# A four-layer graph network on one core: the incidence matrix formed before the transposes, and the transposed adj kept once as fp32

## The chip, the core and the metric

The kernel runs on one core of one Trainium2 chip. TensorE (PE) multiplies, VectorE (DVE) and ScalarE (ACT) do the elementwise work, GpSimd (POOL) does small powers, two reductions over the partitions and the DMAs that add, and SyncE (SP) issues the other DMAs. The metric is the device time of one execution in microseconds (us), the median of several runs.

## What is computed

`x` is 2048x256 in fp32, `adj` is 2048x2048 and sparse, with its diagonal set and entries between 0.05 and 1. Four layers run one after another, each as `x = x + layer(relu(layernorm(x)), adj)`:

```python
# layer 0
deg = sum(adj.T, axis=1); norm = deg**-0.5 [:, None] * adj.T * deg**-0.5 [None, :]
y = norm @ (h @ weight) + bias
# layer 1
head = (adj > 0) / max(sqrt(sum((adj > 0)**2, -1)), 1e-12)
inc = adj + head
y = (inc @ h) / sum(inc, -1)
# layer 2, four heads
ht = (h @ W) per head
e = leaky_relu(src[:, :, None] + dst[:, None, :], 0.01) + adj
y = mean over heads of softmax(e) @ ht
# layer 3
y = relu(adj @ (max(sign(h), 0) @ sign(weight).T))
```

## The kernel before

The 2048 rows are 16 blocks of 128 (`NB`); one block of `adj` against all 16 blocks of columns is a row block. Each product in fp32 is made of fp16 products of high and low parts: a high part is a cast by ACT (times 256 for `adj`), a low part is one instruction of DVE that computes value minus high part. A product of one 128x128 piece takes three matmuls (high·high, high·low, low·high). The order on each engine is the order of the code; semaphores join the engines; nothing is reordered by a scheduler. A block of "loop" code (`Fori`) is run by the engine's sequencer; the rest is unrolled.

- **Load and degrees** (about 0 to 70 us): `adj` comes in as 32 halves of row blocks, ACT and DVE cut it into parts in `nat`, PE sums the degrees.
- **Layer 0** (about 72 to 166 us): for each of 16 row blocks PE runs 48 matmuls (L542 to L544, L552 to L554 for the first two); DVE adds the bias (L1116), takes the sum from PSUM into `x` (L1119), then statistics, relu and the low part `h1_lo` (L1104); ACT makes `h1_hi` (L832) after POOL's power (L438). In the first half DVE also takes a running maximum of `adj` (L1113), from which POOL's reduction over the partitions (L442) gives the shift of the exponential.
- **Layer 1** (166 to 339 us): SP loads `adj` again into `stage` (L330). Per row block and per group of four column blocks (`transpose_group`) PE turns four 128x128 pieces in fp32 (L574); ACT makes the fp16 high part (L848) and `exp(adj - max)` in fp32 (L850) out of PSUM; DVE makes the low part (L1167) and the mask `adj > 0` (L1171). PE then runs, for each of 16 column blocks, five matmuls (`products1`, L594 to L599): three for `adj @ h` and two for `mask @ h`, in two accumulators with a column of ones for the row sums. The sums are combined after the products (`row_counts`, `row_sums`, L1192 to L1208). SP writes the fp16 parts (`adj_t_parts`, L336) and the exponential (`exp_adj_t`, L339) to DRAM, 1 MB each per row block. `h2_transposes` and `scores` (L609, L618) of earlier blocks stand among the products.
- **Between layers 1 and 2** (339 to 398 us): PE forms `ht` for all 16 blocks (`ht_block`, L663, 192 matmuls of 512 columns), ACT and DVE make its high and low parts (L911, L1292). From the scores come the factors `u` and `w`; `u` goes to DRAM and back, spread over all partitions (L359, L362). Behind those loads on SP stands `load_e` (L374), which loads the exponential of four row blocks as 16 pieces into `e_in`.
- **Layer 2** (398 to 741 us): four quarters of the rows times four heads (a "group") times 16 column blocks, 256 steps in all. A step: DVE makes the numerators (L1277), ACT their fp16 high part (L983), DVE the low part (L1282), PE 12 matmuls (L704 to L706). `prob`, `p_hi` and `p_lo` have four slots, so ACT may start on a step when PE is done with the step four earlier (`p_used`). Heads are scaled by ACT (L937) and added to `x` by a DMA of POOL (L460). During quarters 1 to 3 PE, ACT also prepare `xw` of layer 3 (`binary_turn`, `binary_product`).
- **Layer 3** (741 to 805 us): 16 row blocks of 32 matmuls (L745, L746) on the fp16 parts that SP loads back from `adj_t_parts` (L393, L403) into four slots `at3`; DVE adds the result into `x` (L1345), SP writes it out.

## Time and profile before

| what | us |
|---|---|
| median of 3 runs | 808.45 |
| lowest and highest | 804.88, 808.72 |
| the profiled execution, its own time | 806.78 |
| its span (first to last instruction) | 805.0 |
| PE busy in the span | 762.2 (95%) |
| DVE busy | 630.1 (78%) |
| ACT busy | 397.5 (49%) |
| POOL busy | 56.9 (7%) |

The profile is one execution. A matmul's own duration (about 273 ns) overlaps with those around it, so its busy times by line add up to more than the span; what a matmul costs is read from the starts of neighbours. The chain of waits names, for each moment, the instruction that the end of the program waited for.

### The profile page before, as it was taken

The page shows a single profiled execution, that of the slowest core. Times are in us where ns is not written, and L with a number is a line of the kernel's source. Part 1 is how long each engine was busy: PE and PEld are TensorE (multiplying, and loading weights), DVE is VectorE, ACT ScalarE, POOL GpSimd, SP SyncE. Part 2 cuts the span into 40 slices and gives each one's busy share as a digit, 9 for nine tenths or more (in the row PEclk, how much of TensorE's full clock was granted, in tenths as well). Part 3 has the DMA queues.
Part 4 walks back from the last instruction along what each step waited for, and adds up shares of the span by engine and source line. Part 5 has one row for each costly group of instructions (what it writes and reads, how often), then busy time and mean ns, then how long its engine had stood idle before and what let it go on. Part 6 is the DMA issues. An engine that isn't in the chain of part 4 may idle for free.

```text
span 805.0 us, 19016 instructions
## 1 busy us (share of the span) xinstructions
PE 762.2 (95%) x7064; PEld 646.7 (80%) x7064; DVE 630.1 (78%) x1313; ACT 397.5 (49%) x772; POOL 56.9 (7%) x83
## 2 busy tenths in 40 slices
PE   3898998899999999879799999999999999999898
PEld 3665887789999999734488888888888888888687
DVE  6787884867777777646899999999999999996111
ACT  3995100255555555236555555855576555754200
POOL 2002221101101011100000000000000000000000
PEclk9998999999999999979999999999999999999999
DMA  9885002068888887417601181116311490112494
GB/s 336 283 286 177 1 0 104 31 237 292 284 284 298 286 288 239 164 27 211 181 2 28 32 231 28 28 28 180 84 27 28 109 299 18 24 27 80 155 399 178
DMA packets 96716, 120.54 MB, mean 150 GB/s; under 512 B 3537, under 2 KB 82065, under 8 KB 92433
## 3 DMA queue, kind: packets, MB, share of 16 engines
q1 hardware_dynamic: 94496, 111.85, 42.4%
q0 software_dynamic: 2160, 7.87, 5.1%
q8 instruction: 42, 0.69, 0.4%
q14 instruction: 18, 0.14, 0.1%
HBM read 76.15 MB, written 35.68 MB: 139 GB/s over the span
## 4 chain that ended last, share of the span: by engine, by line
PE 76%; DVE 8%; issue 6%; ACT 4%; SPq 3%; DMA 2%; POOL 0%; DVEq 0%; POOLq 0%; ACTq 0%
PE ps L704 14%; PE ps L706 14%; PE ps L705 14%; PE ps L594 4%; PE ps L574 4%; PE ps L596 4%; PE ps L599 3%; PE ps L597 3%; PE ps L595 3%; PE ps L745 3%; PE ps L746 3%; SPq L362 2%; ACT arena L776 1%; DVE arena L1052 1%; DVE arena L1113 1%
## 5 line engine op out<-in xcount | busy, mean ns | idle before, releaser
L704 PE MATMUL ps<-arena 128*128 128x257 f16 x1024 | 279.9, 273 | 2.9 <-DVE arena L1292 2.9
L706 PE MATMUL ps<-arena 128*128 128x257 f16 x1024 | 279.4, 273 | 0.0
L705 PE MATMUL ps<-arena 128*128 128x257 f16 x1024 | 279.2, 273 | 0.0
L983 ACT ACTIVATE arena<-arena 128x512 f16<-128x512 f32 x252 | 158.6, 629 | 136.7 <-PE ps L706 134.7
L1277 DVE SCALAR_TENSOR_TENSOR arena<-arena,w_j 128x512 f32<-128x512 f32 x256 | 190.1, 743 | 0.9 <-DMA arena<-exp_adj_t 0.9
L1282 DVE TENSOR_TENSOR arena<-arena 128x512 f16<-128x512 f32 x256 | 176.3, 689 | 6.1 <-ACT arena L983 5.7
L704 PEld LDWEIGHTS ps<-arena 128*128 128x128 f16 x1024 | 99.9, 98 | 15.9 <-DVE arena L1292 3.4
L705 PEld LDWEIGHTS ps<-arena 128*128 128x128 f16 x1024 | 100.4, 98 | 12.5
L706 PEld LDWEIGHTS ps<-arena 128*128 128x128 f16 x1024 | 99.8, 98 | 12.9
L1167 DVE SCALAR_TENSOR_TENSOR arena<-ps,arena 128x512 f16<-128x512 f32 x64 | 44.0, 687 | 39.9 <-ACT arena L850 39.6
L594 PE MATMUL ps<-arena 128*128 128x257 f16 x256 | 70.3, 275 | 0.0
L599 PE MATMUL ps<-arena 128*128 128x257 f16 x256 | 69.9, 273 | 0.0
L596 PE MATMUL ps<-arena 128*128 128x257 f16 x256 | 69.7, 272 | 0.0
L597 PE MATMUL ps<-arena 128*128 128x256 f16 x256 | 69.7, 272 | 0.0
L595 PE MATMUL ps<-arena 128*128 128x256 f16 x256 | 69.4, 271 | 0.0
L542 PE MATMUL ps<-arena 128*128 128x256 f16 x224 | 61.6, 275 | 2.5 <-DVE x L1119 2.5
L848 ACT ACTIVATE arena<-ps 128x512 f16<-128x512 f32 x64 | 38.1, 596 | 48.1 <-PE ps L574 46.3
L544 PE MATMUL ps<-arena 128*128 128x256 f16 x224 | 61.5, 275 | 0.0
L543 PE MATMUL ps<-arena 128*128 128x256 f16 x224 | 61.5, 275 | 0.0
L745 PE MATMUL ps<-arena 128*128 128x256 f16 x256 | 56.1, 273 | 3.4 <-DMA arena<-adj_t_parts 2.7
L746 PE MATMUL ps<-arena 128*128 128x256 f16 x256 | 56.1, 273 | 0.0
L663 PE MATMUL ps<-arena 128*128 128x512 f16 x192 | 45.9, 404 | 5.0 <-DVE arena L1292 3.4
(148 smaller groups left out, 1082.5 us busy)
## 6 DMA issues: line engine op xcount, KB each, us to landing
arena<-in_adj_dram SPq DMA_DIRECT2D x64, 512.0 KB, 5.5
adj_t_parts<-arena SPq DMA_DIRECT2D x16, 1024.0 KB, 4.6
exp_adj_t<-arena SPq DMA_DIRECT2D x16, 1024.0 KB, 7.8
arena<-exp_adj_t SPq DMA_DIRECT2D x64, 256.0 KB, 4.5
arena<-adj_t_parts SPq DMA_DIRECT2D x16, 1024.0 KB, 7.6
x<-arena POOLq DMA_DIRECT2D x15, 512.0 KB, 5.0
arena<-u_rows SPq DMA_DIRECT2D x4, 1024.0 KB, 14.7
x<-in_x_dram SPq DMA_DIRECT2D x4, 512.0 KB, 5.5
```

The source lines that it names most:

```text
L594: mm(ps[:, 2 * b, 0:DE], at[:, b, 0, j, :], h1_hi[:, j, 0:DE], start=s, stop=False)
L595: mm(ps[:, 2 * b, 0:D], at[:, b, 0, j, :], h1_lo[:, j, :], start=False, stop=False)
L596: mm(ps[:, 2 * b, 0:DE], at[:, b, 1, j, :], h1_hi[:, j, 0:DE], start=False, stop=e)
L597: mm(ps[:, 2 * b + 1, 0:D], mask[:, b, j, :], h1_lo[:, j, :], start=s, stop=False, skip_group_check=True)
L599: ins = mm(ps[:, 2 * b + 1, 0:DE], mask[:, b, j, :], h1_hi[:, j, 0:DE], start=False, stop=e, skip_group_check=True)
L704: mm(ps[:, bank, 0:DE], hi, ht_hi[:, head, j, 0:DE], start=s, stop=False)
L705: mm(ps[:, bank, 0:DE], hi, ht_lo[:, head, j, 0:DE], start=False, stop=False)
L706: ins = mm(ps[:, bank, 0:DE], lo, ht_hi[:, head, j, 0:DE], start=False, stop=e)
L745: mm(ps[:, k, 0:D], at3[:, k, 0, j, :], xw[:, j, :], start=(j == 0), stop=False)
L983: nc.scalar.activation(p_hi[:, j % 4, :], prob[:, j % 4, :], copy).then_inc(p_hi_done, 1)
L1277: v.scalar_tensor_tensor(prob[:, j % 4, :], u_bc[:, h, q * (QB * P):(q + 1) * (QB * P)], w_j[:, j, h:h + 1], e_in[:, j, :], ALU.max, ALU.m ...
L1282: v.tensor_tensor(p_lo[:, j % 4, :], prob[:, j % 4, :], p_hi[:, j % 4, :], ALU.subtract).then_inc(p_lo_done, 1)
```

## The change

- **Layer 1.** SP loads whole rows (`rows`, four buffers of 8 KB per partition). DVE counts the positive entries of a row with one instruction over 2048 columns (`count`: mask and count), POOL takes count^-0.5 (`inverse_count`), and DVE forms `inc = mask * c + adj` with a second instruction over 2048 columns (`fill`), in natural layout. PE turns both `inc` and `adj` in fp32 (eight pieces a group instead of four). ACT makes the fp16 high part of `inc` and copies the turned `adj` in fp32; DVE makes the low part of `inc` (`inc_low`). PE runs three matmuls per column block instead of five, in one accumulator. The row sums take one reciprocal and one instruction.
- **What goes to DRAM.** One fp32 tensor `adj_t`, 1 MB per row block, instead of the fp16 parts and the exponential.
- **Layer 2.** `load_e` loads `adj_t` (512 columns a piece, 16 pieces a quarter); for quarter 0 it stands on SP right behind the end of layer 1 and ahead of the `u` loads. ACT applies the exponential in place (`exp_adj`, 64 instructions of 128x512): four before the exponentials of the scores, six among the `ht` parts, the others among the steps (head 3 of the quarter before, and head 0). The scaling of the last head of a quarter moves from steps 4 to 7 to steps 10 to 13 of the next head 0. The first head's products wait for `ht_lo` column block by column block.
- **Layer 3.** Its fp16 parts are made by ACT (`at3_high`, 128x2048) and DVE (`at3_low`, 128x2048) from `adj_t`: row blocks 0 and 1 inside head 2 of quarters 1 and 2, block 2 and 3 about the end of layer 2, the others inside layer 3.
- **`ht`.** `ht_block` uses three PSUM slots in turn instead of two; blocks 0 to 2 run before the scores' results are back.
- **Layer 0.** The bias is added to `x` by four accumulating DMAs of POOL (from DRAM, spread over partitions) instead of 16 instructions of DVE. `count` and `fill` of the first two row blocks stand in layer 0 (blocks 8 to 11); the transposes of row block 0 stand behind its last four blocks.
- The loops of layers 0, 1, `ht` and 3 are unrolled.

```diff
-    at_dram = nc.dram_tensor("adj_t_parts", (NB, P, 2 * N), F16, kind="Internal").ap()
-    e_dram = nc.dram_tensor("exp_adj_t", (NB, NB, P, P), F32, kind="Internal").ap()
+    adjt_dram = nc.dram_tensor("adj_t", (NB, P, N), F32, kind="Internal").ap()
...
+            sp.wait_ge(l1_ps, NB)
+            load_e(0)
...
             sp.wait_ge(ut_done, 1)
             sp.dma_start(u_dram.rearrange("t h n -> (t h) n"), up_t[0:HEADS * NB, :]).then_inc(u_out, 16)
...
+            pool.wait_ge(relu0, NB)
+            for p in range(4):
+                nc.gpsimd.dma_start(x[:, XP * p:XP * p + XP, :],
+                                    b0_d.partition_broadcast(P).unsqueeze(1).broadcast_to([P, XP, D]),
+                                    accum_op=ALU.add).then_inc(bias_in[p], 16)
...
+            def transpose_group(t, g):
+                n = 4 * t + g
+                if g == 0:
+                    pe.wait_ge(rows_in[t % 4], 16 * (t // 4 + 1))
+                    pe.wait_ge(filled, t + 1)
+                if n >= 2:
+                    pe.wait_ge(adjt_copied, n - 1)
+                    pe.wait_ge(inc_lo_done, n - 1)
...
-                    mm(ps[:, 2 * b, 0:DE], at[:, b, 0, j, :], h1_hi[:, j, 0:DE], start=s, stop=False)
-                    mm(ps[:, 2 * b, 0:D], at[:, b, 0, j, :], h1_lo[:, j, :], start=False, stop=False)
-                    mm(ps[:, 2 * b, 0:DE], at[:, b, 1, j, :], h1_hi[:, j, 0:DE], start=False, stop=e)
-                    mm(ps[:, 2 * b + 1, 0:D], mask[:, b, j, :], h1_lo[:, j, :], start=s, stop=False,
-                       skip_group_check=True)
-                    ins = mm(ps[:, 2 * b + 1, 0:DE], mask[:, b, j, :], h1_hi[:, j, 0:DE], start=False, stop=e,
-                             skip_group_check=True)
+                    mm(ps[:, bank, 0:DE], inc_parts[:, b, 0, j, :], h1_hi[:, j, 0:DE], start=s, stop=False)
+                    mm(ps[:, bank, 0:D], inc_parts[:, b, 0, j, :], h1_lo[:, j, :], start=False, stop=False)
+                    ins = mm(ps[:, bank, 0:DE], inc_parts[:, b, 1, j, :], h1_hi[:, j, 0:DE], start=False, stop=e)
...
+            def exp_adj(q, j):
+                if j % TG == 0:
+                    act.wait_ge(e_loaded[j // TG], 16 * QB * (q + 1))
+                nc.scalar.activation(e_in[:, :, j, :], e_in[:, :, j, :], ACT.Exp, bias=amax[:, 2:3]
+                                     ).then_inc(e_exp, 1)
...
+            h2_turned(NB - 2)
+            h2_high(NB - 1)
+            h2_turned(NB - 1)
+            for j in range(4):
+                exp_adj(0, j)
             act.wait_ge(d_shift, 1)
...
+            def count(t):
+                dve.wait_ge(rows_in[t % 4], 16 * (t // 4 + 1))
+                v.tensor_scalar(mask[:, t % 2, :], rows[t % 4], 0.0, NORM_EPS ** 2, ALU.is_gt, ALU.add,
+                                accum_out=cnt[:, t:t + 1]).then_inc(counted, 1)
+
+            def fill(t):
+                dve.wait_ge(counted, t + 1)
+                dve.wait_ge(c_done, t + 1)
+                if t >= 2:
+                    dve.wait_ge(t_ps, 4 * (t - 2) + 4)
+                v.scalar_tensor_tensor(inc[:, t % 2, :], mask[:, t % 2, :], c_row[:, t:t + 1], rows[t % 4],
+                                       ALU.mult, ALU.add).then_inc(filled, 1)
...
+            def at3_high(i, part, parts=4):
...
+                    if i >= 4:
+                        act.wait_ge(o_ps, i - 3)
...
-                if h == 0 and j % TG == 0:
-                    dve.wait_ge(e_loaded[j // TG], 16 * TG * (q + 1))
+                if h == 0:
+                    dve.wait_ge(e_exp, NB * q + j + 1)
```

On DVE one steady row block of layer 1 read before as below (lines 1167 and 1171 are the low part and the mask of a group, and stand four times in a block):

```order
L1192 TENSOR_SCALAR row_n<-ps 128x1
L1194 TENSOR_SCALAR row_n<-ps 128x1
L1167 SCALAR_TENSOR_TENSOR arena<-ps,arena 128x512
L1171 TENSOR_SCALAR arena<-ps 128x512
L1200 SCALAR_TENSOR_TENSOR row_n<-ps,row_n 128x1
L1202 RECIPROCAL row_n<-row_n 128x1
L1203 TENSOR_SCALAR row_n<-row_n 128x1
L1205 TENSOR_SCALAR row_n<-row_n 128x1
L1206 SCALAR_TENSOR_TENSOR x<-ps,row_n,x 128x256
L1208 SCALAR_TENSOR_TENSOR x<-ps,row_n,x 128x256
```

And so it reads after, on the same engine at the same place (L1234 is `inc_low`, L1220 `count`, L1228 `fill`):

```order
L1234 SCALAR_TENSOR_TENSOR arena<-ps,arena 128x512
L1220 TENSOR_SCALAR arena,cnt<-arena 128x2048
L1234 SCALAR_TENSOR_TENSOR arena<-ps,arena 128x512
L1275 RECIPROCAL row_n<-ps 128x1
L1276 SCALAR_TENSOR_TENSOR x<-ps,row_n,x 128x256
L1228 SCALAR_TENSOR_TENSOR arena<-arena,c_row 128x2048
L1234 SCALAR_TENSOR_TENSOR arena<-ps,arena 128x512
```

The four masks of 512 columns are gone, two instructions of 2048 columns have come in, and the chain of small instructions is shorter by five.

On SP, from the end of layer 1 to layer 2, before:

```order
L336 DMA adj_t_parts<-arena 128x4096
L339 DMA exp_adj_t<-arena 128x16x128
L359 DMA u_rows<-arena 64x128
L362 DMA arena<-u_rows 128x16x128 x4
L374 DMA arena<-exp_adj_t 128x4x128 x64
```

And after, at the same place:

```order
L346 DMA adj_t<-arena 128x2048 x5
L377 DMA arena<-adj_t 128x512 x16
L386 DMA u_rows<-arena 64x128
L389 DMA arena<-u_rows 128x16x128 x4
L395 DMA arena<-adj_t 128x2048 x2
L377 DMA arena<-adj_t 128x512 x48
```

The 16 loads for the first quarter have moved from behind the `u` loads to ahead of them.

## Rows read from the trace of the kernel before

**Rows 1.** The page, parts 1 and 6: engines, then DMA issues, us to landing last.

```profile
PE 762.2 (95%) x7064; PEld 646.7 (80%) x7064; DVE 630.1 (78%) x1313; ACT 397.5 (49%) x772; POOL 56.9 (7%) x83
...
arena<-exp_adj_t SPq DMA_DIRECT2D x64, 256.0 KB, 4.5
...
x<-arena POOLq DMA_DIRECT2D x15, 512.0 KB, 5.0
```

**Rows 2.** Busy time by stretch: length, each engine (instructions), PE clock, DMA share, GB/s.

```profile
72.00:165.90 93.90, 88.34 (x788) 77.98 (x787) 72.91 (x214) 17.18 (x36) 16.59 (x18) 0.98 0.14 52
165.90:339.10 173.20, 172.81 (x1662) 156.25 (x1659) 124.71 (x355) 87.62 (x151) 17.62 (x31) 1.00 0.82 272
339.10:398.10 59.00, 47.36 (x214) 20.53 (x211) 38.10 (x97) 30.66 (x75) 1.53 (x3) 0.91 0.54 143
398.10:740.50 342.40, 342.40 (x3122) 303.92 (x3123) 332.01 (x534) 201.86 (x396) 13.20 (x15) 1.00 0.29 73
740.50:805.00 64.50, 57.94 (x529) 50.78 (x526) 8.79 (x22) 8.32 (x28) 0.00 (x0) 1.00 0.61 228
```

**Rows 3.** The chain in order of time, in layer 1: start, us, what.

```profile
214.95 0.49 PE ps L574 x4
...
225.91 0.49 PE ps L574 x4
...
325.08 0.11 PE ps L594
325.19 0.11 PE ps L595
```

**Rows 4.** Groups by line and shape, DVE and ACT: busy, mean ns, idle before.

```profile
L1167 DVE SCALAR_TENSOR_TENSOR arena<-ps,arena 128x512 f16<-128x512 f32 x64 | 44.0, 687 | 39.9 <-ACT arena L850 39.6
L850 ACT ACTIVATE arena<-ps,amax 128x512 f32<-128x512 f32 x64 | 43.8, 684 | 0.0
...
L1139 DVE CUSTOM_DVE_ANT_0 arena<-arena 128x256 f32<-128x256 f32 x16 | 6.8, 422 | 0.4
...
L1240 DVE SCALAR_TENSOR_TENSOR arena<-arena 128x2048 f16<-128x2048 f32 x1 | 2.3, 2292 | 0.5 <-ACT arena L877 0.5
...
L877 ACT ACTIVATE arena<-arena 128x2048 f16<-128x2048 f32 x1 | 1.9, 1910 | 0.0
...
L1030 DVE TENSOR_SCALAR arena<-arena 128x512 f16<-128x512 f32 x1 | 0.4, 420 | 0.0
```

**Rows 5.** Timeline in layer 0: start, us, engine, line, what, idle before.

```profile
135.33 0.48 DVE L1104 SCALAR_TENSOR_TENSOR arena<-arena,rstd 128x256 f16<-128x256 f32 x1 [9.46 <-ACT arena L832]
```

**Rows 6.** Waits in layer 0: who waited for whom, us in total, times, longest.

```profile
PE ps L574 <- DVE arena L1171: 3.1, 2, 2.6
...
PE ps L542 <- DVE x L1119: 2.5, 2, 2.1
```

**Rows 7.** The chain in order of time, from layer 1 to layer 2.

```profile
339.12 0.17 DVE row_n L1192
...
372.19 4.61 SPq L374
...
379.82 6.08 DMA arena<-exp_adj_t
...
398.10 0.28 PE ps L704
```

**Rows 8.** Timeline of PE in the same stretch: start, us, engine, line, what.

```profile
354.67 33.50 PE L663 MATMUL ps<-arena 128*128 128x512 f16 x144 [1.73 <-DVE arena L1292]
```

**Rows 9.** Timeline of DVE and of ACT in layer 2, columns as in rows 5.

```profile
560.85 0.75 DVE L1277 SCALAR_TENSOR_TENSOR arena<-arena,w_j 128x512 f32<-128x512 f32 x1
561.56 0.69 DVE L1282 TENSOR_TENSOR arena<-arena 128x512 f16<-128x512 f32 x1
...
562.22 0.63 ACT L983 ACTIVATE arena<-arena 128x512 f16<-128x512 f32 x1 [0.69 <-PE ps L706]
```

**Rows 10.** Layer 3: the longest piece of the chain that is no matmul.

```profile
754.90 5.01 DMA arena<-adj_t_parts
```

More of the change, by code:

```diff
@@ L408, in _ @@
+            for t in range(NB - 8, NB):
+                store_out(t)
             sp.wait_ge(out_sent, 16 * NB)
@@ L453, in _ @@
+            for t in range(NB):
+                if t + 2 < NB:
+                    inverse_count(t + 2)
+                if t >= 1:
+                    inverse_root2(t - 1)
+            inverse_root2(NB - 1)
             pool.wait_ge(dmax_part, 1)
@@ new lines, in _ @@
+            pe.wait_ge(deg_copied, 1)
+            for g in range(NB // TG):
+                layer0(NB - 4 + g)
+                transpose_group(0, g)
+            for t in range(NB):
+                for g in range(NB // TG):
+                    if t + 1 < NB:
+                        transpose_group(t + 1, g)
+                    products1(t, g)
+                    if g == 0 and t >= 2:
+                        h2_transposes(t - 2)
+                    if g == 2 and t >= 2:
+                        if t == 2:
+                            pe.wait_ge(wa_done, 1)
+                        scores(t - 2)
@@ new lines, in ht_block @@
+            def ht_block(t):
+                for half in range(2):
+                    if t >= 3:
+                        last = max(k for k in range(t) if HT_SLOT[k] == HT_SLOT[t])
+                        pe.wait_ge(ht_lo_done, HEADS * last + 2 * half + 2)
+                    n = 0
+                    for ha, wb in ((0, w2_hi), (0, w2_lo), (1, w2_hi)):
+                        for c in range(DC):
+                            ins = mm(ps[:, HT_SLOT[t] + half, :], h2_t[:, ha * DC + c, t * P:(t + 1) * P],
+                                     wb[:, c, 512 * half:512 * half + 512], start=(n == 0), stop=(n == 5))
+                            n += 1
+                    ins.then_inc(ht_ps, 1)
@@ L677, in _ @@
+            nc.tensor.transpose(ps[0:HEADS * NB, 6, 0:P], up_i[:, :, :].rearrange("p t h -> p (t h)"),
                                 ident[:, :]).then_inc(ut_ps, 1)
-            with nc.tensor.Fori(1, NB // 2) as i:
-                ht_block(i, False)
+            for t in range(3, NB):
+                ht_block(t)
             def head_products(q, head, first):
@@ L1240, in _ @@
-            v.scalar_tensor_tensor(w2_lo, w2_f, W_SCALE, w2_hi, ALU.mult, ALU.subtract).then_inc(w2_lo_done, 1)
-            with nc.vector.Fori(1, NB // 2) as i:
-                for b in range(2):
-                    layer1(i, b, True)
-            for b in range(2):
-                row_counts(NB - 2 + b, b)
-                row_sums(NB - 2 + b, b)
-                row_norm(NB - 2 + b, b)
-                h2_low(NB - 2 + b, b)
+            for t in range(NB):
+                more = t + 1 < NB
+                if more:
+                    inc_low(t + 1, 0)
+                if t == 0:
+                    w2_a(1, (2, 3))
+                    w2_a_parts()
+                if t + 2 < NB:
+                    count(t + 2)
+                if more:
+                    inc_low(t + 1, 1)
+                if t >= 1:
+                    row_sums(t - 1)
+                if t + 2 < NB:
+                    fill(t + 2)
+                if more:
+                    inc_low(t + 1, 2)
+                if t >= 1:
+                    row_norm(t - 1)
+                if more:
+                    inc_low(t + 1, 3)
+                if t >= 1:
+                    h2_low(t - 1)
+                if t == 0:
+                    dve.wait_ge(w2_hi_done, 1)
+                    v.scalar_tensor_tensor(w2_lo, w2_f, W_SCALE, w2_hi, ALU.mult, ALU.subtract
+                                           ).then_inc(w2_lo_done, 1)
```

789 lines of the change are left out of this document (409 added, 380 removed).

## The prediction

> **What bounds the kernel now.** I read the table of stretches first, then the chain of waits in order of time, then the timelines of the places where the chain leaves PE. PE is busy 762.2 of 805.0 us [rows 1]. By stretch, PE fills layer 1 (172.8 of 173.2 us) and layer 2 (342.4 of 342.4), and has holes in layer 0's end, between layers 1 and 2 (47.4 of 59.0) and in layer 3 (57.9 of 64.5); its clock is full in the three long stretches [rows 2]. So a gain comes either from fewer PE instructions in layer 1 or from closing those holes. In layer 2 DVE is busy 332.0 of 342.4 us and ACT 201.9 [rows 2]: DVE has little to give, ACT much. One matmul starts 0.11 us after its neighbour, four fp32 transposes take 0.44 to 0.49 us of the chain, also 0.11 each, and a row block of layer 1 is 225.91 - 214.95 = 10.96 us long [rows 3]. Check: 80 matmuls and 16 transposes are 96 x 0.11 = 10.6, and `h2_transposes` and `scores` make the rest.
>
> The sum is made against the profiled execution (806.78 us, of which 1.8 lie outside its span); the median of the runs shown is 1.7 above it.
>
> **Layer 1, PE's own work.** Per row block 32 matmuls go and 16 transposes come: 48 x 0.11 + 32 x 0.11 + 0.35 = 9.15, with the bubble that the block of before shows 9.2 us. 10.96 - 9.2 = 1.76, times the 15 blocks that have transposes beside them, is 26.4; the last block has none and saves 32 x 0.11 = 3.5. Together -29.9.
>
> **Layer 1, is DVE fast enough?** Instructions that follow without a wait start about 0.08 us closer than they are long, so a low part of 512 costs 0.61 [rows 4]. Four of them are 2.44. `fill` is a two-input instruction of 2048 with a per-partition factor; L1240, the same without the factor, took 2.29 [rows 4], so 2.3. The reciprocal and the sum into `x` are 0.6, the norm 1.0, `h2_low` 0.4. `count` has no row of its kind: an SBUF-sourced TENSOR_SCALAR of 512 took 0.42 (L1030, 0.52 ns an element and 0.15 fixed), which gives 1.2 us for 2048; the accumulating L1139 took 0.42 for 256, an element per cycle, which gives 2.3 with its read-out [rows 4]. I take 2.3, as the row that also accumulates. DVE then needs 9.05 us a block against PE's 9.15: even. Walking the order of the code, PE's turn of a group waits for the low part two groups earlier and each low part for PE's turn and ACT's cast; with both near 9.15 the walk finds no gap in a steady block, and a POOL power (0.55 us) lies under the `inc_low` between `count` and `fill`. ACT has four casts and four copies of 0.6 and 1.1 more, 5.9 of 9.15. At the start it does not close: in block 0 DVE has in addition two pairs of `w2_a` and `w2_lo` (4.6 us) and no slack, so PE waits about 1.3 us twice. I add 2.6 for that and 1.0 for jitter. If `count` takes 1.2 us, these 3.6 shrink to about 1; if waits leave DVE 0.5 us longer a block, they grow to 10. Layer 1 in all: -29.9 + 3.6 = -26.3 (-29 to -19).
>
> The Trainium skill (VectorE: DVE Perf Modes, section "The perf-mode tier table (the rule you actually need)") lists 1227 ns for a fp32 `tensor_scalar` of 2048 elements in SBUF and says nothing of one that accumulates; by it the sum would be some 2.5 us lower than mine.
>
> **Layer 0.** Removed on DVE: 16 bias adds of 0.42 us, which PE did not wait for. Added: `count` and `fill` twice, in blocks 8 to 11. There DVE sits out POOL's reduction, 9.46 us until 135.33 [rows 5], and PE lost 2.1 us to it, waiting for the sum of block 10 [rows 6]. Now `fill(0)` (2.3) stands in front of that sum, less two bias adds (0.8): a wait of 3.6 instead of 2.1. The 16 more transposes of row block 0 cost 1.8 here. Against this PE's two waits for the low parts and masks of the first turned groups go (3.1 us before [rows 6]), and with them holes of 1.7 about them in which nothing was issued. I count -1.5 for the start of layer 1's products (165.9 before), between -4 and +4. The four bias DMAs start when POOL's powers for the degrees are done, and an adding DMA of this size takes 5.0 us to land [rows 1]; PE's first two sums need 96 x 0.11 = 10.6 us from about the same moment. Covered; if the first lands late, it costs what it is late.
>
> **Between layers 1 and 2.** Layer 1 ended at 339.1, the first product of layer 2 was at 398.1: 59.0 us [rows 7]. The chain ran through the `u` loads, `load_e` behind them (372.2), its landing at 385.9, and then 12 us of numerators and `ht_low` [rows 7]. Afterwards `load_e` is issued at the end of layer 1, 33 us earlier, so it goes off this chain, and PE's `ht` work comes next: 192 matmuls. From the end of layer 1 (E) I count blocks 0 to 2 of `ht`, two `h2_transposes` and `scores` until E+9.4; the return of the scores' factors, which now waits behind four exponentials (4 x 0.68 [rows 4]) that wait for the first 1 MB of `adj_t` (about 6.5 us after E), E+12; then 156 matmuls. 144 took 33.5 us there, with the clock's mean at 0.91 in this stretch [rows 2, 8], so 36 us: E+48. DVE meanwhile follows, and its last `ht_low` and first numerators leave PE waiting some 2.5 us in the first steps. So 50.5 instead of 59.0: -8.5 (-12 to 0; zero if the loads or the factors come as late as before).
>
> **Layer 2.** PE's 12 matmuls a step make 1.32 us, and DVE and ACT keep step with it [rows 9]. ACT waited 0.69 us before each `p_hi` [rows 9]. An exponential from PSUM took 0.684 [rows 4]; two ACT instructions in a row overlap by 0.1, so a step with one is 0.53 + 0.6 = 1.15 of 1.32. It is hidden by ACT's wait, and `p_hi` is only late when a load is late; the loads of the next quarter are issued when its columns are free, five to six steps (7 us) before their exponential, against 4.5 us to landing for 256 KB [rows 1]. DVE gets 8 low parts of 0.61 us for layer 3, four in a row: 2.4 us late, within the three steps that PE has ready. I take +1 for the stretch (0 to +10).
>
> **Layer 3.** PE waited 5.0 us for a load of `adj_t_parts` that could not be issued earlier [rows 10]. Now blocks 2 to 5 are loaded during the last head. The new late one is the cast of block 4: ACT waits for block 0 to leave its slot (`o_ps`), then 1.91 (L877's time), then DVE 2.3 (L1240) [rows 4], while PE has 3 x 0.88 us of work left: a stall of 1.8. Afterwards DVE needs 2.65 a block and ACT 1.9 against PE's 3.5. So -3.2 (-5 to +2).
>
> **Sum.** -1.5 - 26.3 - 8.5 + 1 - 3.2 = -38.5; 806.8 - 38.5 = 768.3. With -1 for the short form of `count`, which I hold possible, I forecast **767 us**.
>
> **Rivals.**
> 1. *DVE bounds layer 1.* If the lag between turn, cast and low part isn't hidden when DVE and PE are both full, a block takes 10.2 us, 15 x 1.0 more: 782. For it: DVE's 9.05 of 9.15. Against: in the walk each low part is ready 0.3 us or more before DVE comes to it.
> 2. *Layer 2 starts no earlier relative to E.* The factors wait behind the exponentials and PE's clock falls in the hole: 776. For it: before, the clock's mean was 0.91 there [rows 2].
> 3. *The exponentials are not hidden in layer 2.* Each adds its own 0.68 to its step through the chain numerators, `p_hi`, low part, next step: 64 x 0.68 = 43.5, which gives 811, slower than before. It decides from 0.6 us each on. Against: 0.69 us of ACT's wait in each step [rows 9].
> 4. *PE's clock falls in layer 1.* At 1.2 GHz, half the clock, a block would be up to 9.2 us longer; five blocks of 16 take the whole gain (above 807), all would give 900. In the block of before 16 of 96 PE instructions were transposes and the clock was 1.00 [rows 2, 3]; now 32 of 80 are. The Trainium skill (TensorE: Matmul & The Clock Gate, section "Part 4: PE-mode transpose") says that transposes do not count as PE being busy in the same way; the trace of before, at full clock with fewer of them, neither shows nor excludes it for this mixture.
> 5. *Better than counted.* `count` short, no wait at the start of layer 1, layer 2 begun at E+47: 759.
>
> **Chances.** Forecast 0.58 (762 to 774), rival 1: 0.12, rival 2: 0.14, rival 3: 0.03, rival 4: 0.03, rival 5: 0.10. The range 756 to 786 leaves out rivals 3 and 4 and the far ends of the others. Faster by over 0.5% (about what a measurement of this kernel can tell from no change) 0.94, within 0.5% 0.01, slower 0.05.
>
> **What would show it.** Layer 1's row blocks 9.1 to 9.5 us apart; `count` 1.2 or 2.3 us; PE idle before the turned groups under 5 us in the stretch; E near 311; first product of layer 2 near E+48 and its steps 1.32 us; one stall of about 2 us in layer 3 before block 4. A block pitch of 10 and more, or PE waiting for low parts in steps with an exponential, would make the prediction wrong.

## The result, and the profile after

The changed kernel takes **771.71 us** (median of four runs, 769.29 to 773.97) where the kernel before took 807.4 beside it: a ratio of 0.956, 95% interval 0.952 to 0.960. Measured again later, on one chip with three of the experiments, it was 0.954 (0.951 to 0.957). Its profiled execution has a span of 768.8 us against 805.0, so 36.2 us went. The forecast of 767 is 4.7 below the median; the median lies inside the range that the forecast gave for its own case (762 to 774).

I cut both profiled executions at five events on PE and DVE (degrees read by DVE, first and last product of layer 1, last product of layer 2, end). Times and changes are in us:

| stretch | before | after | change | forecast |
|---|---|---|---|---|
| start to degrees | 69.4 | 66.2 | -3.2 | 0 |
| to the first product of layer 1 | 96.5 | 93.8 | -2.7 | -1.5 |
| layer 1 | 173.2 | 149.4 | -23.8 | -26.3 |
| end of layer 1 to end of layer 2 | 401.3 | 396.0 | -5.3 | -7.5 |
| rest | 64.6 | 63.4 | -1.2 | -3.2 |

The table of stretches of the kernel after (columns: from and to, then busy us and instructions of PE, of PE's weight loads, of DVE, ACT and POOL, then PE's granted clock, DMA share, GB/s) answers to [rows 2]:

```profile
72.00:160.00 88.00, 85.49 (x783) 76.62 (x781) 67.53 (x188) 13.55 (x28) 14.39 (x22) 1.00 0.36 73
160.00:309.40 149.40, 144.81 (x1383) 130.18 (x1381) 135.14 (x252) 80.60 (x152) 17.09 (x30) 1.00 0.60 198
309.40:360.60 51.20, 44.60 (x215) 19.97 (x213) 31.21 (x80) 33.43 (x79) 0.97 (x2) 0.93 0.59 165
360.60:705.40 344.80, 342.63 (x3122) 303.63 (x3121) 337.47 (x554) 245.05 (x470) 13.06 (x15) 1.00 0.29 79
705.40:768.80 63.40, 57.91 (x530) 50.94 (x527) 39.24 (x36) 30.92 (x40) 0.00 (x0) 1.00 0.55 200
```

In layer 1 PE was full before (172.8 of 173.2); now it is busy 144.8 of 149.4 and DVE 135.1, so something holds PE up. The granted clock stayed at 1.00 there (full speed, 2.4 GHz), with 32 transposes to 48 products in a row block: rival 4 did not happen. Between the layers PE's clock is 0.93 on the mean.

One steady row block of layer 1 on DVE, from its timeline (start, us, engine, line, operation, names and shapes, and in brackets the idle time before it with what ended it); it answers to the sum of durations made from [rows 4]:

```profile
221.32 2.27 DVE L1220 TENSOR_SCALAR_CACHE_REDUCE arena<-arena 128x2048 f16<-128x2048 f32 x1
223.52 0.08 DVE L1220 DVE_READ_ACCUMULATOR arena<-arena 128x1 f32 x1
...
224.72 2.34 DVE L1228 SCALAR_TENSOR_TENSOR arena<-arena,c_row 128x2048 f32<-128x2048 f16 x1
...
228.59 0.68 DVE L1234 SCALAR_TENSOR_TENSOR arena<-ps,arena 128x512 f16<-128x512 f32 x1
229.71 0.48 DVE L1297 SCALAR_TENSOR_TENSOR arena<-arena,row_n 128x256 f16<-128x256 f32 x1 [0.44 <-ACT arena L878]
230.19 0.69 DVE L1234 SCALAR_TENSOR_TENSOR arena<-ps,arena 128x512 f16<-128x512 f32 x1
230.80 2.27 DVE L1220 TENSOR_SCALAR_CACHE_REDUCE arena<-arena 128x2048 f16<-128x2048 f32 x1
```

From one `count` to the next it is 230.80 - 221.32 = 9.48 us. The whole idle time is the 0.44 us ahead of L1297, `h2_low`, which waits for ACT's high part L878, and that for POOL's power of the norm. The waits of DVE and PE in layer 1 as the waits view adds them up (total, times, longest):

```profile
DVE arena L1297 <- ACT arena L878: 7.0, 15, 1.0
PE ps L603 <- DVE arena L1234: 3.1, 3, 1.8
```

Between the layers the chain of waits reads (start, us, what):

```profile
316.68 0.28 DVE dmax L1335
316.96 5.09 issue
322.05 0.40 POOL dmax L488
322.47 0.24 DVE w_j L1339
...
325.26 30.38 PE ps L680 x132
355.66 0.85 ACT arena L943 x2
```

The maximum of d was ready for POOL at 316.96, and POOL's reduction over the partitions began 5.09 us later, though POOL waited for nothing that the profile shows. PE's turn of the scaled scores (L699) waited for it:

```profile
PE ps L699 <- DVE up_i L1343: 4.8, 1, 4.8
PE ps L730 <- DVE arena L1364: 2.2, 2, 1.6
```

### The profile page after: what moved, and what is told of

It reads as the page before. It is cut to its first block, busy times and chain, and to the rows that moved or that the text cites. A ratio compares the mean times of both kernels' runs of the same rounds, so it can differ in the third digit from the quotient of the medians.

```text
span 768.8 us, 16799 instructions
## 1 busy us (share of the span) xinstructions
PE 729.3 (95%) x6808; PEld 619.3 (81%) x6808; DVE 667.2 (87%) x1207; ACT 458.7 (60%) x861; POOL 57.1 (7%) x87
## 4 chain that ended last, share of the span: by engine, by line
PE 72%; DVE 3%; issue 1%; ACT 1%; POOL 0%; ACTq 0%
PE ps L730 14%; PE ps L732 14%; PE ps L731 14%; PE ps L680 5%; PE ps L772 4%; PE ps L773 3%; PE ps L627 3%; PE ps L629 3%; PE ps L628 3%; PE ps L603 3%; PE ps L607 3%; PE ps L641 1%; DVE arena L1228 1%; DVE arena L1371 1%; DVE arena L1234 0%
## 5 line engine op out<-in xcount | busy, mean ns | idle before, releaser
L730 PE MATMUL ps<-arena 128*128 128x257 f16 x1024 | 279.9, 273 | 2.2 <-DVE arena L1364 2.2
L732 PE MATMUL ps<-arena 128*128 128x257 f16 x1024 | 279.4, 273 | 0.0
L731 PE MATMUL ps<-arena 128*128 128x257 f16 x1024 | 279.2, 273 | 0.0
L1037 ACT ACTIVATE arena<-arena 128x512 f16<-128x512 f32 x252 | 158.5, 629 | 95.6 <-PE ps L732 53.2
L627 PE MATMUL ps<-arena 128*128 128x257 f16 x256 | 70.3, 274 | 0.0
L629 PE MATMUL ps<-arena 128*128 128x257 f16 x256 | 69.7, 272 | 0.0
L628 PE MATMUL ps<-arena 128*128 128x256 f16 x256 | 69.4, 271 | 0.0
L574 PE MATMUL ps<-arena 128*128 128x256 f16 x224 | 61.1, 273 | 2.5 <-DVE x L1188 2.5
L576 PE MATMUL ps<-arena 128*128 128x256 f16 x224 | 61.1, 273 | 0.0
L575 PE MATMUL ps<-arena 128*128 128x256 f16 x224 | 61.1, 273 | 0.0
L772 PE MATMUL ps<-arena 128*128 128x256 f16 x256 | 56.1, 273 | 2.5 <-DVE arena L1404 1.8
L773 PE MATMUL ps<-arena 128*128 128x256 f16 x256 | 56.1, 273 | 0.0
L858 ACT ACTIVATE arena<-arena,rstd 128x256 f16<-128x256 f32 x16 | 8.2, 510 | 64.1 <-POOL rstd L458 64.1
L1234 DVE SCALAR_TENSOR_TENSOR arena<-ps,arena 128x512 f16<-128x512 f32 x64 | 43.8, 685 | 2.9 <-ACT arena L869 2.9
L915 ACT ACTIVATE arena<-arena,amax 128x512 f32<-128x512 f32 x64 | 45.0, 708 | 1.3 <-DMA arena<-adj_t 1.3
L680 PE MATMUL ps<-arena 128*128 128x512 f16 x192 | 43.8, 390 | 1.1 <-DVE arena L1371 1.1
```

Source lines behind the costliest of these rows:

```text
L627: mm(ps[:, bank, 0:DE], inc_parts[:, b, 0, j, :], h1_hi[:, j, 0:DE], start=s, stop=False)
L628: mm(ps[:, bank, 0:D], inc_parts[:, b, 0, j, :], h1_lo[:, j, :], start=False, stop=False)
L629: ins = mm(ps[:, bank, 0:DE], inc_parts[:, b, 1, j, :], h1_hi[:, j, 0:DE], start=False, stop=e)
L680: ins = mm(ps[:, HT_SLOT[t] + half, :], h2_t[:, ha * DC + c, t * P:(t + 1) * P], wb[:, c, 512 * half:512 * half + 512], start=(n == 0), st ...
L730: mm(ps[:, bank, 0:DE], hi, ht_hi[:, head, j, 0:DE], start=s, stop=False)
L731: mm(ps[:, bank, 0:DE], hi, ht_lo[:, head, j, 0:DE], start=False, stop=False)
```

## The experiments

Each was run beside the kernel before on one chip, and its ratio is to that. e2 issues the first load of layer 2 later, e3 finishes h2 later in layer 1, e6 leaves `count` out, e16 leaves only its summing out, e9 adds two matmuls a column block, e11 issues the first bias DMA earlier, e12 is e2, e3 and e11 together, e10 is e2 and e3; e14 leaves exponentials out and e15 makes them twice. All these start from the changed kernel; e8 alone starts from the kernel before, with its load issued earlier. Since the stretch up to the degrees moves by itself (below), single stages are compared by the events of the profiled executions. "Row block" is the distance of two row blocks of layer 1 (empty where I did not read it), "way to layer 2" is from the last product of layer 1 to the first of layer 2; the last column is from the last product of layer 2 to the end of the span.

| kernel | ratio to before (95%) | row block | layer 1 | way to layer 2 | layer 2 | rest |
|---|---|---|---|---|---|---|
| before | 1 | 10.96 | 172.9 | 59.3 | 342.1 | 64.8 |
| after | 0.956 (0.952 to 0.960) | 9.48 | 149.3 | 51.3 | 344.6 | 63.6 |
| e2 | 0.949 (0.947 to 0.952) | | 149.3 | 45.3 | 344.6 | 63.6 |
| e3 | 0.948 (0.945 to 0.950) | 9.22 | 145.6 | 49.4 | 344.6 | 63.6 |
| e6 | 0.945 (0.942 to 0.948) | 9.20 | 142.6 | 51.1 | 344.6 | 63.5 |
| e8 | 0.996 (0.995 to 0.998) | | 172.9 | 58.3 | 343.7 | 64.9 |
| e9 | 1.016 (1.014 to 1.017) | 12.70 | 197.7 | 50.8 | 344.6 | 63.5 |
| e11 | 0.955 (0.954 to 0.957) | | 149.3 | 50.1 | 344.6 | 63.6 |
| e12 | 0.946 (0.944 to 0.948) | | 145.7 | 45.7 | 344.6 | 63.5 |
| e14 | 0.952 (0.950 to 0.955) | | 149.3 | 51.3 | 344.6 | 63.6 |
| e15 | 0.977 (0.975 to 0.978) | | 149.3 | 51.0 | 365.9 | 63.6 |
| e16 | one run, 766.7 us | 9.20 | 144.0 | 50.6 | 344.6 | 63.6 |
| e10 | 0.942 (0.940 to 0.944) | 9.22 | 145.7 | 45.5 | 344.6 | 63.6 |

(Layer 1 is given here from the start of its first to the start of its last product, so 0.1 less than above.)

### The changed kernel once more

> The changed kernel as it is, so that the kernels of this group have it beside them on the same chip: 0.956 of the kernel before, within 0.004, about 773 where the kernel before takes 808.8. It also shows how far the end of the load stage moves by itself between executions (the first product of layer 1 came at 160.0 in its first profiled run, and at 159.8 to 162.8 in three variants that leave that stage alone).

Measured: 0.9539, median 772.56 us. The degrees were read at 67.2 and not 66.2, and layer 1 began at 162.3; from there to the end every stage is within 0.4 us of the first profile. So stages can be compared to a few tenths between executions, and the time up to layer 1 only to 2 or 3 us. In ten profiles, of the changed kernel and of its variants that leave the load stage alone, the degrees came at 66.2 to 68.5; of the kernel before there are two, 69.4 (the profile of [rows 1]) and 66.9 (e8). The 3.2 us of the first row of the table is therefore most likely no effect of the change. From the degrees to layer 1 these ten profiles took 93.4 to 95.8 us, against 96.5 and 96.8 (e8) before, so of the second row's 2.7 us only 0.7 to 3.1 can be said.

### Is POOL's late reduction the load's doing? (e2)

```diff
             sp.wait_ge(l1_ps, NB)
+            sp.wait_ge(dmax_all, 1)
             load_e(0)
```

The load is of 4 MB, and not of 2 as the expectation says. And it is not one thing that moves: ACT's first four `exp_adj`, which need this load, move with it, from ahead of the scores' exponentials to among the `ht` parts.

> The changed kernel with one thing moved: the load of the first exponentials' input (2 MB by SyncE's queue) is issued only when GpSimd has given the maximum of d over all partitions, and ScalarE's first exponentials stand some three blocks later. Nothing is left out. In the changed kernel GpSimd stood 10.2 us between its last power and that maximum while this load was landing, against 7.5 us in the kernel before, where it was not. Theory (the load slows GpSimd's change of program): the gap falls to 6 to 7.5 us, the first product of layer 2 comes 3 to 4 us earlier after the end of layer 1, and the time falls by 3 to 4 us against the changed kernel (to about 768). Rival (the gap is GpSimd's own, whatever the queues do): the gap stays at 10 us and the time within 1 us; the exponentials may then even come late for the first product, and cost up to 2 us.

POOL's timeline of the kernel after, and then of e2:

```profile
311.22 0.59 POOL L463 TENSOR_TENSOR row_n<-row_n,neg_half 128x1 f32<-128x1 f32 x1 [4.49 <-DVE row_n L1287]
322.05 0.39 POOL L488 PARTITION_ALL_REDUCE dmax<-dmax  x1 [10.24 <-issue]
```

```profile
313.62 0.58 POOL L464 TENSOR_TENSOR row_n<-row_n,neg_half 128x1 f32<-128x1 f32 x1 [4.50 <-DVE row_n L1286]
320.11 0.39 POOL L489 PARTITION_ALL_REDUCE dmax<-dmax  x1 [5.91 <-DVE dmax L1334]
```

Between power and reduction POOL stood 10.24 us, and now 5.91, as in layer 0 (5.96 in the kernel after). (The 7.5 us that the expectation names for the kernel before ended when DVE's maximum came, so they are no price of POOL's.)

All profiles of the changed kernel and its variants fall in two groups: with the load in flight 8.4 to 10.2 us in nine (DMA share 0.82 to 0.89 over the gap), without it 5.9 to 6.2 in three (e2, e10, e12; DMA share 0.00). A load does not always do this. In layer 0 of the kernel before a load ran too, at a share of 0.52, and the gap was 6.1. In e8 (below) the same 4 MB were issued 1.2 us after the power, the share over the gap was 0.60, and the reduction began at 348.62, 0.1 us after the maximum was ready: POOL's own part was 7.5 us at most there. ACT's four exponentials, which e8 does not have at this place, began at 317.21 in the kernel after, inside POOL's gap; no run moves them alone, so that it is the load and not they is likely and not shown. What POOL does in that time (it changes from a power to a reduction) the profile does not name; POOL's queue shows two MODIFY_POOL_CONFIG at the start of the gap (312.0 in the kernel after, 314.4 in e2).

The way to layer 2 fell by 6.0 us, more than the 4.4 that PE's wait lost (4.8 to 0.4). The rest is in the `ht` products that follow. Tables of stretches, after and then e2, over the hole and over the same 132 products:

```profile
309.40:325.00 15.60, 9.26 (x59) 4.27 (x56) 4.78 (x20) 6.46 (x15) 0.97 (x2) 0.90 0.79 270
325.00:355.50 30.50, 30.24 (x133) 13.39 (x134) 21.82 (x52) 23.66 (x58) 0.00 (x0) 0.94 0.59 139
```

```profile
311.80:323.00 11.20, 9.13 (x59) 4.24 (x56) 4.71 (x20) 3.85 (x11) 0.97 (x2) 1.00 0.10 20
323.00:352.00 29.00, 28.68 (x133) 13.05 (x134) 21.81 (x52) 25.33 (x62) 0.00 (x0) 1.00 0.75 234
```

The granted clock was 0.90 and 0.94 of full speed on the mean with PE's wait of 4.8 us, and 1.00 without it. Cut finer, it was 0.50 (1.2 GHz) from 322 to 327 and 1.00 from 329, with PE idle from 318.9 to 323.7 and for 1.1 us more until 325.3. The products took 30.4 us of the chain and then 28.7. The wait cost 4.4 us and the clock behind it another 1.7. The exponentials in their later place put nothing on the way to layer 2. Against the changed kernel the time fell by 0.5 to 0.7%, some 5 us.

### Does the 0.44 us wait for `h2_low` matter? (e3)

`h2_low(t - 1)`, which stood last in DVE's turn t, behind its fourth `inc_low`, is now `h2_low(t - 2)` behind `count(t + 2)`; ACT's `h2_high`, PE's `h2_transposes` and `scores` move later likewise.

> The changed kernel with the finishing of each row block of h2 (high part on ScalarE, low part on VectorE, transposes on TensorE) put one to three groups later in each engine's order of layer 1, so that VectorE no longer stands 0.44 us a block for ScalarE's high part behind GpSimd's power. Nothing is left out. Theory (VectorE bounds the block of 9.48 us: 9.05 busy and 0.44 of wait): the block falls to 9.1 to 9.2 us, 16 blocks give 4 to 5 us, about 767. Rival (TensorE bounds it, 8.86 us of matmuls and what its sequencer adds): the block stays at 9.4 or more, and the time within 1 us.

The row blocks are 9.22 us apart and layer 1 is 3.7 us shorter. PE's transposes of h2 in the timeline of PE (one line a block) show the distance:

```profile
205.21 0.39 PE L641 MATMUL ps<-ident,arena 128*128 128x128 f16 x4
214.43 0.39 PE L641 MATMUL ps<-ident,arena 128*128 128x128 f16 x4
223.65 0.39 PE L641 MATMUL ps<-ident,arena 128*128 128x128 f16 x4
```

So the theory held for layer 1. Another 1.9 us came on the way to layer 2, where POOL's gap was 8.6 us and PE's wait 2.6 instead of 4.8 us; I had not expected that, and no run shows why the gap was shorter.

### What lies under DVE's limit? (e6, e16, e9)

e6 leaves `count` out from row block 2 on, e16 only its summing:

```diff
-                v.tensor_scalar(mask[:, t % 2, :], rows[t % 4], 0.0, NORM_EPS ** 2, ALU.is_gt, ALU.add,
-                                accum_out=cnt[:, t:t + 1]).then_inc(counted, 1)
+                    v.tensor_scalar(mask[:, t % 2, :], rows[t % 4], 0.0, None, ALU.is_gt)
+                    v.tensor_copy(cnt[:, t:t + 1], cnt[:, t - 2:t - 1]).then_inc(counted, 1)
```

> The changed kernel with VectorE's count of the incidence entries of a row (2.28 us and 0.08 of accumulator read, once a block) left out for 14 of the 16 row blocks; a copy of one column stands in its place, so the counts in the output are wrong, and nothing else is left out. Theory (VectorE bounds the block): it has 6.8 us of work left, so the block falls from 9.48 to TensorE's own time, 8.86 to 9.1 us, and the time by 6 to 9 us, to 763 to 766. Rival (TensorE and its waits bound the block already): the block stays within 0.1 us and the time within 2 us.

> The changed kernel with the sum taken out of VectorE's count in 14 of the 16 row blocks: the comparison of 2048 elements is still made and written, but not summed, and an older count stands in its place, so that the counts in the output are wrong. The summing form took 2.28 us and 0.08 for its read-out. Theory (the summing makes it an element per cycle): the plain comparison takes 1.0 to 1.3 us, and the block falls from 9.48 to about 8.9, as when the count is left out. Rival (2.28 us is the price of reading 2048 fp32 values with a comparison): it stays at 2.2 or more, and the block above 9.3.

Both have row blocks of 9.20 us: taking 2.4 us a block from DVE gives 0.28, hardly more than taking away its wait of 0.44 in e3 (0.26). Below 9.2 TensorE is the bound: from 200 to 230 us PE is busy 30.00 of 30.00 us in e6, e16 and e3, and 29.66 in the kernel after. That is above the 8.86 I had expected here and exactly the 9.2 that the prediction worked out with its bubble. What e6 gains over e3 (3.0 us in layer 1) is at the layer's start, where PE's waits for low parts went from 3.1 to 0.5 us:

```profile
PE ps L603 <- DVE arena L1237: 0.5, 1, 0.5
```

The groups of DVE in e16 and then in the kernel after (busy, mean ns) settle what `count` pays for:

```profile
L1224 DVE TENSOR_SCALAR arena<-arena 128x2048 f16<-128x2048 f32 x14 | 17.0, 1217 | 0.0
```

```profile
L1220 DVE TENSOR_SCALAR_CACHE_REDUCE arena<-arena 128x2048 f16<-128x2048 f32 x14 | 31.9, 2275 | 0.0
```

The comparison alone is 1217 ns for 2048 elements, the summing form 2275. Both prices that the prediction had from neighbours, 1.2 and 2.3, were right, each for its form.

e9 puts two more matmuls of 256 columns into each column block:

```diff
+                    mm(ps[:, bank, 0:D], inc_parts[:, b, 1, j, :], h1_lo[:, j, :], start=False, stop=False)
+                    mm(ps[:, bank, 0:D], inc_parts[:, b, 1, j, :], h1_lo[:, j, :], start=False, stop=False)
```

> The changed kernel with five matmuls a column block in layer 1 and not three: two more of 256 columns, whose sums spoil the result and are of no use (the low part of h1 times the low part of the matrix, twice). VectorE's and ScalarE's work is as it was. In the kernel before, five stood there. Theory (a matmul of 256 columns costs 0.11 us of a TensorE that has 8.86 us of work a block, against VectorE's 9.49): 32 more a block are 3.52 us, the block goes to 12.4, and layer 1 takes 46 to 50 us more, about 819 to 822; with the slack of 0.6 us a block counted only once. Rival (the gain of the change came from VectorE's shorter block, and TensorE has more room than it seems): less than 40 us more.

The block went to 12.70: 3.50 more than PE's own 9.20, which is 32 x 0.11. Layer 1 took 48.4 us more, and the kernel became slower than the one before. So the change gains by the two products that it removes; with its transposes and its other work but all five products it would be a loss.

### Was it the load of the exponentials' input? (e8)

```diff
             sp.wait_ge(l1_ps, NB)
             sp.wait_ge(h2_lo_done, NB)
+            load_e(0, True)
             sp.wait_ge(ut_done, 1)
...
-            for q in range(NQ):
-                load_e(q, q == 0)
+            for q in range(1, NQ):
+                load_e(q, False)
```

> The kernel before with one part of the change alone: the load of the first exponentials' input is issued at the end of layer 1, ahead of the six DMAs that spread u, and not behind them. Nothing is left out. The recorded theory puts a piece of the chain between layers 1 and 2 on this load (issued at 372.2, landed at 386.0, first product at 398.1) and would have the first product come up to 8 us earlier, about 800. Rival, from a closer look at the same trace: the transposed h2 was complete at 385.1, 0.9 us before this load landed, so that the load was only one of two that came late together, and its move alone gives 0 to 1.5 us, about 806 to 807; what gave the rest in the changed kernel was the shorter way of h2.

In the kernel before, DVE's first numerators waited only 0.88 us for the load (DVE's timeline):

```profile
386.00 1.41 DVE L1277 SCALAR_TENSOR_TENSOR arena<-arena,w_j 128x512 f32<-128x512 f32 x2 [0.88 <-DMA arena<-exp_adj_t]
```

In e8 the load was issued 13 us ahead of the first `u` DMA and was off the chain, and the way to layer 2 still took 58.3 us instead of 59.3. From the first product of layer 1 to the end of the span it is 639.8 us, and 639.1 in the kernel before. The 1 us was lost again at once: in both kernels PE waited 2.87 us ahead of its first product of layer 2, but in e8 the granted clock was at half behind that wait, where it was 1.00 in the kernel before, and layer 2 took 1.6 us more (343.7 against 342.1). From 394.9 to 398.4 us the clock of e8 was 0.54.

The median is 3.0 us lower (0.2 to 0.5%), more than this. In the profiles the rest lies ahead of layer 1 (its first product comes at 163.7 and not 165.9), where this edit changes nothing, and I leave it open. Up to 8 us it is not. What ends that way instead stands in its last steps: in e8 the chain of waits goes through PE's `ht` work (28.4 us from 352.43) and not through the load. First e8, then the kernel after (DVE's and PE's timeline):

```profile
382.87 1.40 DVE L1279 SCALAR_TENSOR_TENSOR arena<-arena,w_j 128x512 f32<-128x512 f32 x2
384.31 1.35 DVE L1284 TENSOR_TENSOR arena<-arena 128x512 f16<-128x512 f32 x2
385.69 3.23 DVE L1294 SCALAR_TENSOR_TENSOR arena<-ps,vp_j,arena 128x256 f16<-128x256 f32 x8
388.83 1.41 DVE L1279 SCALAR_TENSOR_TENSOR arena<-arena,w_j 128x512 f32<-128x512 f32 x2
390.28 1.35 DVE L1284 TENSOR_TENSOR arena<-arena 128x512 f16<-128x512 f32 x2
391.67 3.22 DVE L1294 SCALAR_TENSOR_TENSOR arena<-ps,vp_j,arena 128x256 f16<-128x256 f32 x8
394.95 0.40 PE L706 MATMUL ps<-arena 128*128 128x257 f16 x1 [2.87 <-DVE arena L1294]
```

```profile
357.32 1.41 DVE L1357 SCALAR_TENSOR_TENSOR arena<-arena,w_j 128x512 f32<-128x512 f32 x2
358.76 1.36 DVE L1364 TENSOR_TENSOR arena<-arena 128x512 f16<-128x512 f32 x2
360.16 1.66 DVE L1371 SCALAR_TENSOR_TENSOR arena<-ps,vp_j,arena 128x256 f16<-128x256 f32 x4
```

Before, PE waited for all 64 low parts of `ht`, and DVE put numerators twice and 16 low parts in front of that: 12.1 us from 382.87. In the kernel after PE waits for those of its own column block, and with three PSUM slots only the last two blocks stand among the numerators: the first product comes at 360.6, 3.3 us after 357.32, and follows PE's own `ht` work without a hole. That is 8.8 us less. At the front of the way the maximum of d was ready 7.7 us after the last product of layer 1 and not 11.9 (348.5 in e8), and POOL's gap of 5.1 us took that back. PE then waited 2.2 us for low parts in the first steps, where DVE is busy 7.7 of 7.8 us; that is the 2.5 us by which layer 2 became longer. No run isolates these two lines of the change, so this is read from the traces and not tried.

### Are the exponentials hidden in layer 2? (e14, e15)

e14 cuts 48 of 64 exponentials to one column, e15 makes them twice.

> The changed kernel with 48 of its 64 exponentials, those of the second to fourth quarter of layer 2 (0.71 us each on ScalarE, 34 us together), cut to one column; the attention weights of these rows are then wrong, and nothing else is left out. Theory (they are hidden under TensorE's 1.32 us a step): layer 2 stays at 344.6 us between its first and last product and the time within 1 us of the changed kernel's, 772. Rival (part of them is exposed): the time falls by what they cost, up to 34 us.

> The changed kernel with the same 48 exponentials made twice, the second on the output of the first; the weights of these rows are then wrong, and nothing is left out. A step with one holds ScalarE for about 1.15 us of TensorE's 1.32; with two it is 1.8 to 2.0. Theory (the exponential is hidden only because one fits the step): the steps with two are 0.5 to 0.7 us late, less what the three steps in TensorE's reserve take up in each of the nine runs of four to eight such steps: 10 to 30 us more, 782 to 802, with TensorE waiting for low parts there. Rival (ScalarE's 37% of idle time in layer 2 takes them up): under 3 us.

Leaving 34 us of ACT's work out changes layer 2 by 0.0 us in the profiles; the ratio, 0.952, is a little below the two of the changed kernel (0.954 and 0.956), with intervals that overlap theirs. Doubled, it adds 21.3 us to layer 2, inside the 10 to 30 of the theory. ACT's timeline of e15 where each step has two (L917 and L920), L1042 being `p_hi`:

```profile
445.56 0.62 ACT L1042 ACTIVATE arena<-arena 128x512 f16<-128x512 f32 x1
446.08 0.71 ACT L917 ACTIVATE arena<-arena,amax 128x512 f32<-128x512 f32 x1
446.82 0.72 ACT L920 ACTIVATE arena<-arena,amax 128x512 f32<-128x512 f32 x1
447.45 0.61 ACT L1042 ACTIVATE arena<-arena 128x512 f16<-128x512 f32 x1
```

A step is 447.45 - 445.56 = 1.89 us where PE needs 1.32, although ACT has much idle time over the layer, in the kernel after 95.6 us ahead of its `p_hi`:

```profile
L1037 ACT ACTIVATE arena<-arena 128x512 f16<-128x512 f32 x252 | 158.5, 629 | 95.6 <-PE ps L732 53.2
```

One exponential is free, two are not: room is counted by the step and not by the layer. Rival 3 did not happen with one exponential a step; with two, 0.57 us a step is exposed, near the 0.6 from which on it would have decided.

### The bias DMA (e11), and what adds up (e12, e10)

e11 issues the first of the four bias DMAs before the powers of the degrees; e12 is e2, e3 and e11 together, e10 is e2 and e3.

> The changed kernel with the first of the four bias DMAs of layer 0 issued by GpSimd before its powers of the degrees, and not behind them. Nothing is left out. In the changed kernel this DMA was issued at 70.6, landed 5.5 us later, and VectorE waited 2.5 us for it, TensorE 2.5 us behind VectorE. Theory: that wait goes, and layer 0 ends 1.8 to 2.5 us sooner after the degrees, if the powers, which the first product needs, start no later. Rival: the issue takes GpSimd 1 us or more ahead of the powers, layer 0 starts that much later, and the net is within 1 us either way.

> The changed kernel with three moves at once: the load of the exponentials' input behind the maximum of d (alone 3.6 us in the profiled runs, 0.9491 of the kernel before against 0.956), the finishing of h2 put later in layer 1 (alone 5.8 us, 0.9475), and the first bias DMA ahead of the powers (not yet known alone, 0 to 2.5). Nothing is left out. If they add up: 9 to 12 us below the changed kernel, 761 to 764 where that takes 773. If two of them compete for the same wait (the second shortens GpSimd's gap to 8.6 us by itself, 1.6 of its gain): 7 to 9 us, 764 to 766.

> The changed kernel with two moves at once: the load of the exponentials' input behind the maximum of d, and the finishing of h2 put later in layer 1; the bias DMAs stay where the changed kernel has them. With the third move, the first bias DMA ahead of the powers, it was 0.9456 of the kernel before, and layer 1 took 145.7 us, the way to layer 2 45.7. If the third move gives nothing on balance, this is the same within 0.2%: 763 to 764.5 where the kernel before takes 807.6. If it gave 1 to 2 us, this is 765 or more; if it cost 1 to 2, 762 or less.

In the kernel after, the bias DMAs landed later than the 5.0 us of [rows 1]; the view of their line gives:

```profile
DMA to landing us min/median/max: 10.2/18.5/29.3
```

The waits of PE for DVE's sums in layer 0, and then in e11. In the kernel after, the 1.8 us is behind the bias DMA (DVE waited 2.5 for it), the other 0.7 behind `fill(0)`:

```profile
PE ps L574 <- DVE x L1188: 2.5, 2, 1.8
```

```profile
PE ps L578 <- DVE x L1192: 0.5, 2, 0.3
PE ps L521 <- DVE arena L1126: 5.6, 2, 5.3
```

The wait behind the DMA went, as the theory had it, and another came that neither theory had: the DMA, issued at 51.0, now ran while the input was still loading. In the 7 us from 56 to 63 its packets of 1 KB took 45.4% of the DMA engines' time for 0.41 of 1.82 MB. Queue, kind, packets, MB, share of 16 engines' time:

```profile
q1 hardware_dynamic: 375, 1.39, 58.8%
q0 software_dynamic: 415, 0.41, 45.4%
```

ACT waited up to 5.3 us for a piece of `adj` (2.4 us in four waits in the kernel after, 6.4 in e11), and the degrees came at 70.6 instead of 66.2 to 68.5; in e12 at 69.9. From the degrees to layer 1 it took 91.6 us (91.8 in e12) instead of 93.4 to 95.8. On balance it gave nothing in e11.

So e10, without it, is the best version: **761.59 us, 0.942 (0.940 to 0.944)**, against 0.9456 (0.9437 to 0.9475) for e12 and 0.954 to 0.956 for the changed kernel. By the two ratios the early bias DMA costs some 3 us beside the other two moves; the intervals just touch. By stage the parts add up but for one: layer 1 takes 145.7 us as in e3, the way to layer 2 45.5 as in e2, and the 1.9 us that e3 gained on that way is no gain on top of e2's 6.0.

## Why the prediction was right, point by point

The total was near, and in part by chance. In the pair of profiles three terms came out smaller than forecast: layer 1 by 2.5 us, the stretch from its end to the end of layer 2 by 2.2, the rest by 2.0. Against these 6.7 us stand 3.2 us at the start, which no term had and which is most likely variation, and 1.2 more in layer 0, inside the variation of that stretch too. The -1 for a short `count` did not come either: `count` took 2.28 us. What was right is where the gain would be: 23.8 of the 36.2 us are in layer 1, from fewer matmuls.

- **Layer 1, PE's work**: right. PE's own block is 9.20 (e6, e16), as worked out, and e9 gives 0.11 for a matmul.
- **Layer 1, DVE**: the 9.05 us of work is right (9.48 less the wait of 0.44), and the 2.3 for `count`. The step that failed is the walk that "finds no gap in a steady block": it looked at turn, cast and low part, and not at `h2_low`, which waits for POOL's power and ACT's high part, 0.44 us a block. With DVE nearly full only 0.16 of it was taken up, and the block became 9.48 instead of 9.20. As in rival 1 DVE then sets the block, but by another wait than the lag that rival 1 names, and by a quarter of its 1.0 us; e3 removes it. The waits at the start were put at 2.6 and measured 3.1.
- **Layer 0**: right within its bounds, for other reasons. The wait behind `fill(0)` was put at 3.6 us and measured as 0.7; the bias DMA that the prediction called covered landed late and cost PE 1.8.
- **Between the layers**: the size was near (-5.3 with layer 2's first steps, against -8.5), the mechanism was not. The step that failed is that the load "goes off this chain" and so gives the gain: the load was one of two works that ended nearly together, DVE waited for it 0.88 us and no more, and without it the way is 1.0 us shorter (e8). By the traces the gain is the shorter end of `ht`; that is read and not tried. The missing 3 us are POOL's reduction, which began at E+12.7 while the whole return of the factors was put at E+12, and the clock behind the hole. Both went when the load and ACT's first exponentials were put later (e2). The part of rival 2 that says the clock falls in the hole happened: it was 0.50 from 322 to 327.
- **Layer 2**: right. The +1 was 0: the exponentials cost nothing (e14), and the 2.5 us more of the layer are the first steps, which the term before has.
- **Layer 3**: the new stall of 1.8 us was measured at 1.77 (answering to [rows 10]):

```profile
724.13 0.28 PE L772 MATMUL ps<-arena 128*128 128x256 f16 x1 [1.77 <-DVE arena L1404]
```

The term was mis-sized by the old stall: the 5.0 us are the DMA's piece of the chain, but PE stood only for 2.7 of them, since it still had work while the DMA ran. 2.7 - 1.8 = 0.9, and 1.2 was measured.

## What to carry to other kernels

A long piece of the chain is not a gain to be had. What its removal gives ends where the next work was ready anyway, so look up when each of the works that meet at its end was done; here that was 0.9 us apart. When two engines are both nearly full, walk every wait of the fuller one through a block, small ones too: here 0.44 us a block on DVE made each block 0.26 us longer, and without it layer 1 was 3.7 us shorter (e3), where forecast and time were 2.5 apart. A DMA that is moved ahead meets other work: the early bias DMA delayed the input, and with the early load POOL's step from one kind of work to another took longer. In neither case did the earlier place gain anything over the later one.

## What the runs showed of the hardware

- POOL stands 5.9 to 6.2 us between a power and a reduction over partitions with a DMA share of 0.00 to 0.01 over that time (e2, e10, e12, and layer 0 of the kernel after), and also 6.1 with 0.52 (layer 0 of the kernel before). It was 7.5 at most with 0.60 (e8), and 8.4 to 10.2 with 0.82 to 0.89, where a load of 4 MB was in flight and, inside the gap, ACT's exponentials began.
- A summing comparison of 2048 fp32 elements takes 2275 ns on DVE, the plain one 1217. The Trainium skill (VectorE: DVE Perf Modes, section "The perf-mode tier table (the rule you actually need)") gives 1227 for the plain one, and e16's 1217 agrees with that; the form that sums took 1.9 times as long.
- With one hole of 4.8 us in PE's work the granted clock was 0.50 from 322 to 327 us and 1.00 from 329, which cost 1.7 us over 132 products of 512 columns. Behind a hole of 2.87 us it was 0.54 for 3.5 us in e8 and 1.00 in the kernel before, so the length of that hole alone did not decide it. 32 fp32 transposes among 80 matmuls and transposes left the clock at 1.00 for 149 us.
- An adding DMA of 0.5 MB in packets of 1 KB, issued by POOL during the load of the input, made the degrees come at 69.9 (e12) and 70.6 (e11) instead of 66.2 to 68.5, 1.4 to 4.4 us later.
